# Statistics of four late blocks in a gated-delta-rule layer: from VectorE to ScalarE

## The reference, cut to what matters

```python
xn = _layernorm(x)                       # x is (16, 512, 256): 8192 rows of 256
x = x + attn(xn) + moe(xn)
# attn: a second layernorm of xn, projections q, k, v, beta, g, then for each of 512 time steps, 16 heads, 16 batches:
Sst = Sst * g_t
kS  = einsum('bhk,bhkv->bhv', k_t, Sst)
Sst = Sst + b_t * einsum('bhk,bhv->bhkv', k_t, v_t - kS)
o_t = einsum('bhk,bhkv->bhv', q_t, Sst)
# then the output projection, a layernorm and an MLP
# moe: router, top 8 of 64 experts, 64 expert MLPs of width 192, one shared expert MLP
```

## Time and profile before

| | us |
|---|---|
| median of 3 runs | 1914.68 (1905.7 to 1916.29) |
| the profiled execution | 1918.32 |
| its span, first to last instruction | 1916.6 |
| VectorE busy | 1742.9 (91%) |
| GpSimd busy | 1589.8 (83%) |
| TensorE busy | 1446.8 (75%) |
| ScalarE busy | 911.6 (48%) |

### The profile page before, as it was taken

One profiled execution on the slowest core, in us unless ns is written; L12 is line 12 of the kernel. 1 busy time (PEld: TensorE's weight loads), 2 busy tenths in 40 slices (PEclk: granted clock), 3 DMA queues, 4 the chain that ended last, 5 costly groups with the idle time before them and its releaser, 6 DMA issues. The chain is left out here.

```text
span 1916.6 us, 31509 instructions
## 1 busy us (share of the span) xinstructions
PE 1446.8 (75%) x8846; PEld 1255.2 (65%) x8846; DVE 1742.9 (91%) x4967; ACT 911.6 (48%) x2609; POOL 1589.8 (83%) x1343
## 2 busy tenths in 40 slices
PE   6776778877863676675666759898888899888858
PEld 5666667766752565564555648786777778767657
DVE  3599999999999999999988998999999999998980
ACT  3545455556554545555533356455553444433313
POOL 5369999798998879888898888998899999987861
PEclk9878778778875877787877679998999999979879
DMA  8685344544347567856568422242223311111111
GB/s 167 151 184 113 75 95 110 134 92 95 88 113 166 130 139 174 203 127 165 128 167 225 91 51 59 79 122 69 64 58 101 85 54 52 61 54 46 44 42 25
DMA packets 337169, 201.24 MB, mean 105 GB/s; under 512 B 208226, under 2 KB 327716, under 8 KB 336996
## 3 DMA queue, kind: packets, MB, share of 16 engines
q1 hardware_dynamic: 318724, 168.43, 35.9%
q0 software_dynamic: 15616, 30.55, 7.2%
q10 hardware_dynamic: 2656, 0.26, 0.1%
HBM read 127.58 MB, written 71.60 MB: 104 GB/s over the span
## 5 line engine op out<-in xcount | busy, mean ns | idle before, releaser
L826 POOL TENSOR_TENSOR rp<-S,qs 128x2048 f32<-128x2048 f32 x113 | 520.1, 4602 | 76.5 <-DVE S L1143 56.5
L1128 DVE SCALAR_TENSOR_TENSOR vwin<-S,gwin,bank 128x256 f32<-128x256 f32 x1024 | 485.4, 474 | 0.3
L1143 DVE SCALAR_TENSOR_TENSOR S<-S,gwin,bank 128x256 f32<-128x256 f32 x1024 | 484.8, 473 | 0.3
L1133 DVE TENSOR_REDUCE nu<-vwin 128x16 f32<-128x272 f32 x1024 | 439.8, 429 | 0.3
L1137 DVE TENSOR_TENSOR bank<-nu,bank 128x256 f32<-128x256 f32 x1024 | 432.3, 422 | 0.6
L1778 PE MATMUL bank<-region 128*128 128x128 f32 x2048 | 283.4, 297 | 0.0
L1778 PEld LDWEIGHTS bank<-region 128*128 128x128 f32 x2048 | 268.2, 211 | 18.5 <-issue 17.9
L834 POOL TENSOR_TENSOR r<-rp 128x1024 f32<-128x1024 f32 x113 | 273.6, 2421 | 7.0
L1658 PE MATMUL bank<-xaT,wqkvg 128*128 128x128 f32 (+1 forms) x1792 | 243.8, 289 | 11.8 <-ACT xaT L1317 8.5
L1789 PE MATMUL bank<-region 128*128 128x256 f32 x1024 | 235.5, 384 | 0.0
L1658 PEld LDWEIGHTS bank<-xaT,wqkvg 128*128 128x128 f32 (+1 forms) x1792 | 217.3, 191 | 27.0 <-ACT xaT L1317 12.3
(11 more groups left out here) (160 smaller groups left out, 2373.6 us busy)
## 6 DMA issues: line engine op xcount, KB each, us to landing
qkv_d<-stg SPq DMA_DIRECT2D x192, 128.0 KB, 2.3
region<-in_L_ffn_w_gate SPq DMA_DIRECT2D x64, 192.0 KB
region<-in_L_ffn_w_up SPq DMA_DIRECT2D x64, 192.0 KB
region<-in_L_ffn_w_down SPq DMA_DIRECT2D x64, 192.0 KB
region<-in_L_attn_x SPq DMA_DIRECT2D x16, 512.0 KB, 8.6
region<-in_L_attn_x SPq DMA_DIRECT2D x32, 256.0 KB, 4.8
xw_d<-region SPq DMA_DIRECT2D x32, 256.0 KB, 3.5
acc_d<-region SPq DMA_DIRECT2D x32, 256.0 KB, 4.4
```

The costliest lines, as they stand in the source:

```text
L826: g.tensor_tensor(rp[:, :, :].rearrange("p (a v) d -> p a v d", v=DH), S[h][:, lo:lo + HS].rearrange("p t s (v d) -> p (t s) v d", v=DH), ...
L1128: m[G] = mark(v.scalar_tensor_tensor(products_of(I, s, G)[0], earlier(h, s, G).rearrange("p (v d) -> p v d", v=DH), gwin[:, I // NB2 & 1, ...
L1133: m[G] = mark(v.tensor_reduce(nu[:, G], products_of(I, s, G)[1], AX.X, ALU.add))
L1143: ins = v.scalar_tensor_tensor(S[h][:, s, G], earlier(h, s, G), gwin[:, I // NB2 & 1, G, 1, t:t + 1], outer[G], ALU.mult, ALU.subtract)
```

## The change

The code for the statistics of blocks 4 to 7 leaves VectorE's list and enters ScalarE's. For each tile ScalarE runs two passes over the 256 columns: a Copy scaled by -1/256 whose running sum is the negative mean, and a Square with that as its bias whose running sum is 256 times the variance. Each pass waits for the one before it (`late_avg`, `late_dev`), since both write one scratch tile `dev`. Half a block (4 tiles) is done in each of the iterations 0 to 7: in iteration 0 all four behind the last output copy, in iterations 1 to 7 two behind the first Silu and two behind the fourth. For blocks 5 to 7 ScalarE waits until `stats_done` has counted the block before. GpSimd makes the factors of block 4, 5, 6, 7 in iterations 1, 3, 5, 7, with one small operation replaced by another, and SyncE loads blocks 5, 6, 7 in iterations 2, 4, 6.

```diff
+        dev = carve(D)
...
-                if 2 <= I < 2 + LATE:
-                    sp.wait_ge(xs_used, I + 3)
-                    load_xs(sp, I + 3)
+                if I % 2 == 0 and 1 <= I // 2 <= LATE:
+                    sp.wait_ge(xs_used, I // 2 + 4)
+                    load_xs(sp, I // 2 + 4)
...
                 pool.wait_ge(xs_used, k + 1)
+                if k < 4:
+                    g.tensor_scalar(nmean[:, lo:hi], mean[:, lo:hi], -1.0, None, ALU.mult)
+                else:
+                    link(g.tensor_scalar(var[:, lo:hi], var[:, lo:hi], 1.0 / D, None, ALU.mult))
                 link(g.tensor_scalar(tmp_st[:, lo:hi], var[:, lo:hi], 1.0 + EPS, EPS * EPS, ALU.mult, ALU.add))
-                g.tensor_scalar(nmean[:, lo:hi], mean[:, lo:hi], -1.0, None, ALU.mult)
...
-                    if 1 <= I <= 1 + LATE:
-                        front_factors(I + 3)
-                        route_factors(I + 3)
+                    if I % 2 and I // 2 <= LATE:
+                        front_factors(I // 2 + 4)
+                        route_factors(I // 2 + 4)
...
-                    if 1 <= I <= 1 + LATE and s >= 5:
-                        late_stats(I + 3, s - 5, t_)
...
+            def late_stats(I, lo, hi):
+
+                k, half = 4 + I // 2, I % 2 * (NB2 // 2)
+                act.wait_ge(xs_ld[4], 32 * (k - 3))
+                if k > 4:
+                    act.wait_ge(stats_done, k)
+                for q in range(half + lo, half + hi):
+                    done, n = (k - 4) * NB2 + q, k * NB2 + q
+                    act.wait_ge(late_dev, done)
+                    a_.activation(dev, xs[4][:, q, :], ACT.Copy, scale=-1.0 / D,
+                                  accum_out=nmean[:, n:n + 1]).then_inc(late_avg, 1)
+                    act.wait_ge(late_avg, done + 1)
+                    a_.activation(dev, xs[4][:, q, :], ACT.Square, bias=nmean[:, n:n + 1],
+                                  accum_out=var[:, n:n + 1]).then_inc(late_dev, 1)
+                if half and hi == NB2 // 2:
+                    act.wait_ge(late_dev, (k - 3) * NB2)
+                    act.sem_inc(xs_used, 1)
...
                 unit_silu(q, 0)
+                if it <= 2 * LATE + 1:
+                    late_stats(it, 0, 2)
                 unit_evac(q + 1)
...
                 unit_silu(q + 3, 3)
+                if it <= 2 * LATE + 1:
+                    late_stats(it, 2, NB2 // 2)
                 if I + 1 < NRT:
                     route_norm(I + 1, I + 1, 1 - h)
...
                     front_vg(f, h)
+                if I < R0:
+                    late_stats(I, 0, NB2 // 2)
```

## The result

The changed kernel takes 1961.66 us (median of 4 runs, 1960.37 to 1963.36) against 1915.49 for the kernel before in the same comparison (4 runs, 1905.70 to 1921.48). The ratio is 1.025, 95% interval 1.0227 to 1.0273: slower. Forecast were 1952 us and a range of 1932 to 1964; of the loss, 37 us were forecast and 46 measured. The profiled execution took 1960.90, its span 1959.2, 42.6 more than before.

A forecast was written before the change was run, and what follows sets the result against it. The prediction took VectorE's list as the bound, with ScalarE in a tight ring with TensorE and VectorE. Iterations 1 to 7 grow from 210.3 to 247.4 us, so 1914.7 + 37 = 1952 us, range 1932 to 1964.

The forecast's parts named there:

- The ring: ScalarE, TensorE and VectorE wait on each other from Silu 0 to Silu 0, 26.0 us, about 1 us slack per iteration.
- A tile's price: Two dependent ScalarE passes per tile cost 0.55 + 0.60 = 1.15 us; 32 pairs add 37 us to ScalarE.
- Iteration 1: Waiting 5.2 us for block 4 plus pairs of 4.6 move Silu 0 from 109.97 to 119.8; length 42.2 us.
- The wait for the factors: In iterations 2, 4, 6 ScalarE waits for GpSimd's bias until 12.5 us into the iteration, a stall of 4 us.
- The 8.4 us that the prediction set for Silu 0: Silu 0's place in an iteration, taken as product 0 at 8.84 us less 0.42; starts the odd iterations' sum.
- the prediction's sum for those pairs: Two pairs behind Silu 3 add nothing: next Silu 0 comes 14.0 us behind it, VectorE gets there 14.1 behind.
- The sum: Iterations 1 to 7: 42.2 + 3 x 36.6 + 3 x 31.8 = 247.4 us against 210.3, a loss of 37.
- the clock: TensorE's unit 1 runs slow after the gap behind unit 0: 2.1 us in even iterations, 1.05 in odd ones.
- The left-out squares and roots: ScalarE's squares and roots at the ends of iterations 2, 3, 4 could add up to 2 us; not counted.
- If VectorE stays the bound this is the gain: Statistics, aggregates and copies leaving VectorE save 3.5 us a block, 14 us for four.
- the first rival: VectorE stays the bound, ScalarE's passes fit its idle time: 1914.7 - 14 = 1901 us; chance 0.07.
- Rival 3: Slower only in part, one stall short or some given back later: +21 to +27, 1935 to 1941 us; chance 0.22.

The follow-up runs named there:

- pairs_before_silu0: Changed kernel without the stats_done wait, the two pairs behind Silu 0 in iterations 1 to 7 put ahead of it; 1927.55 us, ratio 1.0059 to the kernel before.
- spread: Changed kernel without the stats_done wait or passes in iteration 0, passes put at five places where ScalarE waits; 1920.99 us, ratio 1.0026 to the kernel before.
- no_factor_wait: Changed kernel without ScalarE's wait for stats_done in iterations 2, 4 and 6, nothing else; 1948.67 us, ratio 1.0208 to the kernel before.
- the dosed filling: Changed kernel with unread matmuls in TensorE's gap behind unit 0, 9 in odd and 27 in even iterations; 1949.16 us, ratio 1.0176 to the kernel before.
- no_late_stats: Kernel before with VectorE's statistics of blocks 4 to 7 replaced by copies of block 0's; 1911.66 us, ratio 0.9988.
- the deferred versions: Three of four front_factors operations moved to iterations 9, 11, 13, 15, in spread (1920.98 us, ratio 1.0021) and in the kernel before (1917.67 us, 1.0008).
- light_factors: no_late_stats with GpSimd's seven factor operations per block replaced by four small copies; 1903.02 us, ratio 0.9928 to the kernel before.

## Why the prediction was right, and where it was off

**The ring.** Right. The loss comes from the order on ScalarE, evacuation to unit to Silu to product, and not from ScalarE's load. `pairs_before_silu0` and `spread` make the same passes as `no_factor_wait` and lose 21 and 28 us less by iteration 8; the first of them differs from it in nothing but the place.

**A tile's price.** 1.15 us forecast, 1.17 measured (the first pass of one pair at 106.55, of the next at 107.72).

**Iteration 1.** Silu 0 forecast at 119.8, measured 118.73. The span of before and after differ in where iteration 1 starts, 100.95 and 99.37, so counted from there it was 18.85 and is 19.36. Length 42.2 forecast, 42.95 measured.

**The wait for the factors.** Forecast 12.5 us into the iteration; in iteration 2 it ended 155.00 - 142.32 = 12.7 into it. `no_factor_wait` shows it to be a cause and not only a row. The 8.4 us that the prediction set for Silu 0 are no reading of it, however: 8.84 is where product 0 stands in VectorE's list, and Silu 0 of iteration 7 is at 290.19, which is 5.96 us into it. With two pairs behind Silu 3 the changed kernel has Silu 0 at 7.74 to 10.23, so the number did for another reason, the one given in the prediction's sum for those pairs.

**The sum.** Lengths of iterations 1 to 7, from the key copies:

| | 1 | 2 | 3 | 4 | 5 | 6 | 7 | sum |
|---|---|---|---|---|---|---|---|---|
| before | 30.6 | 31.0 | 30.7 | 31.6 | 29.3 | 30.2 | 26.4 | 209.7 |
| forecast | 42.2 | 36.6 | 31.8 | 36.6 | 31.8 | 36.6 | 31.8 | 247.4 |
| after | 43.0 | 37.4 | 34.1 | 37.5 | 34.1 | 37.5 | 31.2 | 254.8 |

Iteration 7 ends here at the first of two copies that the view shows as one row, 0.3 us ahead of the second, in both kernels. The forecast is 7.4 us short here, most of it in iterations 3 and 5. **The mis-sized term is the clock.** I took half of 2.1 us in odd iterations, since the gap of 2.5 us lay between a row of 2.92 with a slow clock and one of 1.36 with a fast one. The gap came out at 2.09, and the clock was slow all the same. I had placed the gap behind a rise of the clock; that is so in iteration 7, where it fell over the gap, but in 3 it had not risen yet, and in 1 and 5 it fell only in the unit. In all I charged 4 x 1.05 + 3 x 2.1 = 10.5 us for it; the dosed filling gives 15.3. That is 4.8 of the 7.4. By place it is this: from Silu 0 to Silu 1 the odd iterations lost 6.1 us to the clock, not 4.2, and the even ones 5.5, not 6.3; and 3.8 were lost from Silu 1 to Silu 2, where I had charged nothing. That stretch took 5.3 to 5.8 us in iterations 1 to 6 instead of 5.04, with the projection at 2.42 instead of 1.95. So the greater part is not the half that I took but a place that I left out. The left-out squares and roots are the next: they stand ahead of Silu 0 in iterations 3 and 5, which falls at 9.13 and 10.23 us instead of 8.4, 2.6 together. Iteration 8 is 29.7 instead of 28.35, where I had said that nothing differs. That was wrong. In the changed kernel ScalarE has no wait for GpSimd there; its Silu 0 stands 8.95 us into the iteration instead of 7.00, and VectorE waits 1.22 us for Silu 3. The rows point to the pairs behind Silu 3 of iteration 7, which no run took out alone.

**"If VectorE stays the bound this is the gain", 14 us.** Wrong, though it does not enter the sum, whose new lengths were built from the ring. With the statistics removed altogether the ratio is 0.9988, some 2 us, and 6 at most by the interval. I had seen that GpSimd "would soon have met" a shorter iteration and still gave the first rival 14 us. GpSimd was no second bound to come but already at the limit: its readings were 31.8 us apart before, and those from 183.33 to 271.06 us came without any wait. The first rival was therefore not only unlikely but, as `no_late_stats` shows, out of reach at its price; at best it was "no change". The rule of the Trainium skill that I weighed there ("Perfetto Trace Analysis", section "Optimizing Scalar/DVE Operations": when DVE is saturated, it may make sense to offload some work to Scalar) says no more than "may". Here the runs say no twice: on the ring (ratio 1.025) and, with the ring avoided, on the third engine (1.0026).

**Rival 3**, smaller losses because one stall is short or is given back, did not happen: the loss at iteration 56 is 44.0, of 45.1 at 8. That all is carried to the end is what the forecast assumed. It is no law of this kernel, as the deferred versions show, which lost 6 to 8 us of gain by iteration 17.

**Open.** What `spread` loses behind iteration 24 (from +0.6 there to +7.3) lies in stages that no edit touched, and was not tracked down. `no_late_stats` and `light_factors` move by 6 and 5 us the same way between iterations 24 and 40, so scatter between executions may be much of it. For the wait for the factors the traces and the ratios differ by a factor of two.

## What to carry to other kernels

Before work is moved to a half-idle engine, write down whom its next instruction feeds: idle time ahead of an instruction that waits for a neighbour is free, idle time behind one that a neighbour waits for is not, and by that place alone the same passes differed by 21 us. Then take the work out altogether and time that; it gives the most that any move can bring, and here it would have ended the matter at 0.9988. Where two engines both show 90% or more, look at each iteration's list on each before one of them is called the bound.

## What was not expected of the hardware

In iteration 3 TensorE's granted clock was 0.50 on both sides of a gap of only 2.09 us, though the engine had worked from 184.26 to 189.69 ahead of it; it was 1.00 only in the work behind unit 1 (197.6 to 199.0). Filling the gaps with matmuls of 0.23 us each brought the next unit from 2.86 to 3.67 us down to 1.94, and the changed kernel gained 14 us by work that nobody reads. And a running sum costs ScalarE a read of the accumulator of 0.19 us behind each pass, so that passes of 0.42 and 0.51 us make 1.17 us a pair.
